# Transposing expert rows in 32 bits, later weight splits, tanh gates and a predicated last stage in a one-core transformer stack

## The reference

```python
# first block: attention with a distance bias, then 16 experts, tw = routing weights (at most 2 of 4 groups, 2 of 4 experts in each)
for e in range(E):
    h = jax.nn.silu(xf @ W1[e]) * (xf @ W3[e])          # 128 -> 512
    out = out + tw[:, e:e + 1] * (h @ W2[e])            # 512 -> 128
# second block: two recurrent layers of width 256 over 126 steps, then a dense layer
    i = jax.nn.sigmoid(g[:, 0 * h_dim:1 * h_dim])       # g = x_t @ Wx + b + h @ Wh
    f = jax.nn.sigmoid(g[:, 1 * h_dim:2 * h_dim])
    c_tilde = jnp.tanh(g[:, 2 * h_dim:3 * h_dim])
    o = jax.nn.sigmoid(g[:, 3 * h_dim:4 * h_dim])
    m_new = jnp.tanh(g[:, 4 * h_dim:5 * h_dim])
    c_new = f * c + i * c_tilde
    h_new = o * jnp.tanh(c_new) + m_new
  return jnp.einsum('bth,ho->bto', h2, Wfc) + bfc
# and 8 experts, one for each token
idx = jnp.argmax(logits, axis=-1)
for e in range(num_experts):
    h = jax.nn.relu(xf @ W1[e] + b1[e])                 # 128 -> 256
    y = h @ W2[e] + b2[e]                               # 256 -> 128
    out = jnp.where((idx == e)[:, None], y, out)
```

## Time and profile before

| | us |
|---|---|
| three timed runs | 1154.62, 1159.3, 1160.98; median 1159.3 |
| profiled execution | 1149.07, its span 1147.2 |
| granted clock of PE, mean of the span | 0.902 of 2.4 GHz |
| busy: PE, DVE, ACT, POOL | 916.4, 834.9, 627.2, 351.2 |
| routing | 176 to 247 |
| tile loop | 247 to 513 |
| gathering and mixing the experts' rows | 513 to 540 |
| recurrence, dense layer | 540 to 1003, 1003 to 1014 |
| last stage | 1014 to 1147 |

### The profile page before, as it was taken

The page is one execution under the profiler, slowest core; times in us unless marked ns, Lnnn a source line. Parts: engine busy times, 40 slices in busy tenths (PEclk is TensorE's granted clock), DMA queues, the critical chain, the costliest instruction groups (busy, mean ns, idle before and its releaser), DMA issues.

```text
span 1147.2 us, 44932 instructions
## 1 busy us (share of the span) xinstructions
PE 916.4 (80%) x17542; PEld 726.7 (63%) x17542; DVE 834.9 (73%) x2906; ACT 627.2 (55%) x1954; POOL 351.2 (31%) x483
## 2 busy tenths in 40 slices
PE   4767777258878778874599999999999999689887
PEld 1346545135555545552589899898899888646665
DVE  3458975986666665666788888888888888646998
ACT  0446668226666666653355555555555555436775
POOL 0326646766666655640000000010000010011221
PEclk9768987559999999995699999999999999778999
DMA  8600014202222211216000000000000000003231
GB/s 239 252 1 2 1 44 151 59 21 61 63 63 65 61 49 52 40 35 168 2 4 0 0 0 0 0 0 0 0 0 0 0 0 0 2 1 129 91 112 51
DMA packets 26713, 52.13 MB, mean 45 GB/s; under 512 B 4529, under 2 KB 17817, under 8 KB 26649
## 3 DMA queue, kind: packets, MB, share of 16 engines
q1 hardware_dynamic: 21656, 41.04, 10.9%
q0 software_dynamic: 4992, 10.23, 3.4%
HBM read 44.02 MB, written 7.24 MB: 45 GB/s over the span
## 4 chain that ended last, share of the span: by engine, by line
PE 30%; DVE 13%; issue 11%; ACT 0%; DVEq 0%; POOL 0%; DMA 0%; POOLq 0%; ACTq 0%
PE quad L1332 18%; PE bank L1332 7%; DVE hidL L1711 4%; DVE post L1471 3%; DVE post L1507 2%; DVE area L1725 1%; DVE post L1513 1%; DVE post L1508 1%; PE quad L1392 1%; PE quad L1342 1%; PE quad L1616 1%; PE bank L1627 0%; PE bank L341 0%; PE bank L1621 0%; PE quad L319 0%
## 5 line engine op out<-in xcount | busy, mean ns | idle before, releaser
L1332 PE MATMUL quad<-post,area 128*128 128x32 f16 (+1 forms) x7520 | 231.6, 183 | 29.6 <-DVE post L1513 22.9
L1332 PEld LDWEIGHTS quad<-post,area 128*128 128x128 f16 x7520 | 214.3, 97 | 44.4 <-DVE post L1513 44.4
L1332 PE MATMUL bank<-post,area 128*128 128x32 f16 (+1 forms) x6260 | 193.5, 180 | 6.3 <-DVE post L1513 4.1
L1332 PEld LDWEIGHTS bank<-post,area 128*128 128x128 f16 x6260 | 177.2, 96 | 12.0 <-DVE post L1513 4.6
L1410 ACT ACTIVATE post<-post 128x64 f32<-128x64 f32 x252 | 64.6, 257 | 160.5 <-DVE post L1471 160.5
L1315 POOL COPY post<-post 128x32 f32 (+1 forms) x126 | 26.5, 210 | 386.2 <-DVE post L1513 386.2
L856 POOL DMA_INDIRECT y_scratch<-area x78 | 85.3, 1094 | 80.1 <-DVE area L1216 66.2
L1497 DVE SCALAR_TENSOR_TENSOR post<-post 128x32 f32<-128x32 f32 x252 | 48.5, 192 | 75.2 <-ACT post L1421 75.2
L937 PE MATMUL quad<-const,area 128*128 128x128 f16 x624 | 55.1, 221 | 48.0 <-DVE area L1203 34.2
L851 POOL DMA_INDIRECT area<-x_scratch,area x78 | 81.8, 1049 | 27.6 <-issue 22.2
L937 PEld LDWEIGHTS quad<-const,area 128*128 128x128 f16 x624 | 40.3, 98 | 78.7 <-DVE area L1203 40.5
(11 more groups left out here) (258 smaller groups left out, 2150.7 us busy)
## 6 DMA issues: line engine op xcount, KB each, us to landing
w0s<-in_w SPq DMA_DIRECT2D x12, 768.0 KB, 12.0
area<-mask_scratch SPq DMA_DIRECT2D x7, 1008.0 KB, 4.7
area<-in_rec SPq DMA_DIRECT2D x7, 640.0 KB
post<-y_scratch SPq DMA_DIRECT2D x16, 252.0 KB
area<-in_w SPq DMA_DIRECT2D x4, 768.0 KB
post<-in_f SPq DMA_DIRECT2D x8, 256.0 KB, 4.5
area<-in_patches SPq DMA_DIRECT2D x1, 1488.4 KB
area<-in_taps SPq DMA_DIRECT2D x1, 1350.0 KB
```

What stands on the lines that cost most here:

```text
L1332: mm = pe.matmul(at[0][:, at[1] + out.start:at[1] + out.stop], rec_w[:, w, s, m * P:(m + 1) * P], operand, start=False, stop=False, skip_g ...
```

## The change

- **Tile loop.** `hid` is transposed as it is, in 32 bits: four transposes in place of eight, into one of two banks by turns. ACT writes the high half from PSUM (`high`), and DVE the low half as PSUM minus the high half (`low`), both straight to `hidT`. ACT's L1014 and DVE's L1210 are gone, and `low` reads PSUM.
- **Late splits.** Experts 12 to 15 are split inside the tile loop, behind tiles 2, 5, 8 and 11, all by ACT and DVE; PE waits for them before tile 32. The recurrent weights' splits start at tile 14 in place of 6, each in two instructions for an engine in place of one, because the columns of the gates i and f get half the scale. `rows_low` moves into the table loop.
- **Gates.** sigmoid(x) is taken as (1 + tanh(x/2))/2, with the halving in weights and bias: one tanh of 96 columns in place of a sigmoid of 64 and a tanh of 32. The cell is kept doubled.
- **Dense layer.** Three of its four blocks are multiplied inside the last steps of the recurrence (`connect`, `FC_AFTER`).
- **Last stage.** The mask product is gone. `down` adds up only over one expert; when a block is done, DVE copies it by predicate, under the token mask, to `xn` (`pick_own`, 32 copies). Bias products are added to the stream apart. The mask's transposes come behind the first three `up`. Block results are added to the stream as they come (`finish`).

```diff
@@ tile loop, PE @@
-                for s, (ready, turned, name) in enumerate((("hid_high", "turned0", "turned_ps0"),
-                                                           ("hid_low", "turned1", "turned_ps1"))):
...
+                pe.wait_ge(sg("gated"), i + 1)
+                if i >= 2:
+                    pe.wait_ge(sg("hid_low"), i - 1)
+                for c in range(C0):
+                    mm = pe.transpose(hidT_bank[i % 2][:, c * P:(c + 1) * P], hid[:, i % 2, c * P:(c + 1) * P], ident)
+                mm.then_inc(sg("turned_ps0"), 1)
             def down(i, weights):
-                pe.wait_ge(sg("turned0"), BATCH + i + 1)
-                pe.wait_ge(sg("turned1"), BATCH + i + 1)
+                pe.wait_ge(sg("hid_low"), i + 1)
@@ tile loop, DVE @@
             def low(i):
                 dve.wait_ge(sg("hid_high"), i + 1)
-                if i >= 2:
-                    dve.wait_ge(sg("turned_ps1"), BATCH + i - 1)
-                dve.tensor_tensor(hid16[:, i % 2, 1, :], hid[:, i % 2, :], hid16[:, i % 2, 0, :], ALU.subtract
+                dve.tensor_tensor(hidT[:, i % 2, 1, :], hidT_bank[i % 2], hidT[:, i % 2, 0, :], ALU.subtract
@@ splits, ACT and DVE @@
-            for e in range(2 * EARLY, E0):
-                w_high(act, e)
...
+                if late_tile(i) is not None:
+                    w_high(act, late_tile(i))
...
-            for e in LOW_DVE[3:]:
-                w_low_dve(dve, e)
-            rows_low(0)
-            rows_low(1)
...
-                if c == 8 or c == 16:
-                    rows_low(2 + c // 16)
+                if c % 4 == 0 and c < 4 * NBLK:
+                    rows_low(c // 4)
@@ recurrence @@
+        FC_AFTER = {SEQ - 1: ((0, 0),), SEQ + 1: ((0, 1),), SEQ + 2: ((1, 0), (1, 1)), SEQ + 3: ((2, 0), (2, 1))}
...
-                act.activation(gates[:, l, SIG:2 * SW], pre[:, l, 0:2 * SW], ACT.Sigmoid, scale=UNSCALE)
-                act.activation(gates[:, l, CAND:CAND + SW], pre[:, l, 2 * SW:3 * SW], ACT.Tanh, scale=UNSCALE
+                act.activation(gates[:, l, 0:3 * SW], pre[:, l, 0:3 * SW], ACT.Tanh, scale=UNSCALE
@@ last stage, DVE @@
-                    dve.tensor_tensor(fhid[:, k % 2, :], relu[:, k % 2, :], blk(mask_b[:, u], k // C1), ALU.mult
-                                      ).then_inc(sg("masked"), 1)
...
+            def pick_own(e, j, u, half):
...
+                dve.wait_ge(sg("f_down"), e * ITEMS1 + (j + 1) * C1)
...
+                dve.copy_predicated(xn_blocks[j], blk(mask_b[:, u], j).bitcast(I32), bank[j][:, 0:BLK]
+                                    ).then_inc(sg("picked"), 1)
...
+                    if k in (5, 7):
+                        pick_own(e, (k - 5) // 2, u, half)
...
+                    if k in (1, 3) and not first:
+                        pick_own(e - 1, (k + 3) // 2, 1 - u, half + u - 1)
```

More of the change, by code:

```diff
@@ L1232, in ffn_dve @@
                 if 1 <= i <= NT:
-                    turned_low(i - 1)
+                    low(i - 1)
+                if late_tile(i - 1) is not None:
+                    w_low_dve(dve, late_tile(i - 1))
                 w = rec_tile(i - 1)
@@ L1420, in cell_of @@
                 act.wait_ge(sg(f"cell{l}"), n)
[L1421 removed]
+                act.activation(tanh_c[:, l], gates[:, l, CELL:CELL + SW], ACT.Tanh, scale=0.5).then_inc(sg(f"tanh_c{l}"), 1)
             def both(t, u):
@@ L1555, in build @@
         ITEMS1 = NBLK * C1
+        LN4_BANKS = [bank[i] for i in (*FC_BANK, 4)]
         ln4_high, ln4_low = split_x("ln4")
@@ L1640, in expert @@
                     n = e * ITEMS1 + k
+                    if first and k == LAG:
+                        turn_mask()
                     if k == 0:
@@ L1678, in expert @@
                         act.wait_ge(sg("f_bias"), e + 1)
+                    if first and k == LAG:
+                        mask_rows()
                     act.wait_ge(sg("f_up"), n + 1)
-                    if not (first and k < 2):
-                        act.wait_ge(sg("masked"), n - 1)
-                    act.activation(relu[:, k % 2, :], bank[4 + k % 4][:, 0:BLK], ACT.Relu,
+                    if not (first and k < 4):
+                        act.wait_ge(sg("f_hid_low"), n - 3)
+                    act.activation(relu[:, k % 4, :], bank[4 + k % 4][:, 0:BLK], ACT.Relu,
                                    bias=f_bias[:, u, c:c + 1]
@@ L1732, in last_dve @@
-            for j in range(NBLK):
-                dve.tensor_tensor(st_blocks[j], st_blocks[j], bank[j][:, 0:BLK], ALU.add).then_inc(sg("final"), 1)
+            for j in range(NBLK // 2, NBLK):
+                pick_own(E1 - 1, j, 1, E1 // 2 - 1)
+                finish(j)
         block = ctx.enter_context(nc.Block())
```

196 lines of the change are left out of this document (108 added, 88 removed).

## The result

Four executions gave 1110.15 to 1119.23 us, median 1117.6, against 1158.94 for the kernel before (four executions): the ratio is 0.9636 (95% interval 0.9592 to 0.968), some 41 us less by the medians. The profiled execution took 1110.15 us, its span is 1108.2.

What follows compares the result with a forecast made beforehand. PE was taken as the nearest bound in the tile loop and recurrence, DVE as ahead in routing and last stage. 6.8 + 30 + 1 + 5 + 8.1 = 51 us off the median 1159.3 gave 1108, range 1085 to 1142.

Steps and rivals of the forecast that it cites:

- Tile loop: Tile loop: 32-bit transposes remove PE's 33.9 us wait behind DVE's low half; net of splits 30 us less.
- a sign of being wrong that I had named: Tile loop: gated products staying 3.2 us apart or more, with idle time put down to "remote" before ACT's high half.
- The first rival: Tile loop: the wait moves and the pace mostly stays; 10 of 34 us won, splits take 4, total 1132; chance 0.20.
- PE's order costs nothing: Tile loop: PE's transposes cost the same, half as many of the dearer 32-bit ones coming to about 0.5 us.
- Late splits: Tile loop: four splits of 1.75 us on DVE, partly hidden by its slack, cost 4 us, between 2.6 and 7.
- The later recurrent splits: Tile loop: the same work in more instructions, covered by DVE's and ACT's slack, cost 0.
- Routing: Before the tile loop: chain 6.2 us earlier, L1116 1.5 shorter, row halves charged 0.9; 6.8 us less, between 5 and 8.
- Recurrence: Recurrence: one tanh saves only in the first and last four passes; 1 us less, between 0 and 2.
- Dense layer: Behind the recurrence: twelve of 16 records move into PE's idle time in the last steps; 5 us less, 2.6 to 6.8.
- the half clock: Dense layer: if the half clock stays for the records put into the last steps, only 2.6 us is left.
- Last stage: Last stage: head 2, end 1.1, and 5 of PE's 8.9 us wait behind DVE's low part; 8 us less, 3 to 12.
- The copy's low price: Last stage: each copy by predicate costs DVE 0.67 us; the rival price of 1.35 gives total 1113, chance 0.05.

Runs made afterwards that it cites:

- the pieces: Changed kernel with every weight split of the tile loop cut into three pieces in three successive tiles; 1063.6 us, 0.9684 of the kernel before.
- the last two groups: Eight follow-up runs on one further chip, among them both unchanged kernels; there the kernel before took 1098.7 us and the changed kernel 1070.8.
- the experiment: Changed kernel with the last stage of before (masked products, mask's transposes and bias products first, four adds at the end); 1086.2 us, 0.9884 of the kernel before.

## Why the prediction was right, and where it was not

**The total and its sign.** 1117.6 lies in the range (1085 to 1142), 10 us above the forecast. It came out near by two errors of opposite sign, which is luck: the tile loop gave 5 us in place of 30, and the other stages 34 in place of 21. The profile met a sign of being wrong that I had named: the starts are 3.24 us apart in the mean, over 3.2, with idle time put down to "remote", though ahead of ACT's token copy and of `keep` and not of ACT's high half.

**Tile loop, the step that failed.** I read PE's 33.9 us of idle time behind DVE's low half as the price of where `low` stood, and took them all off. The same kernel shows what it was: on a chip without held releases its loop takes 204.3 us, so that some 50 of its 255 us were held releases, which surfaced mostly at that wait. The changed kernel has them too and pays them at the next wait, `keep`: 47.6 us. The first rival had this mechanism and, for the loop, its size (10 won, 4 for the splits, 6 net; 5.4 measured); its total of 1132 missed by what the other stages gave. What the transposes are worth by themselves is 5 to 8 us where nothing is held, and most of it lies beside the splits: a recurrent weight's three tiles take 8.7 us with the 32-bit transposes (3.0, 3.0, 2.7) and 9.2 in the kernel before (3.2, 3.3, 2.7), while the undisturbed pace is 2.5 in both; on the first chip they were not tried apart from the splits. That PE's order costs nothing was right: 2.50 us a tile undisturbed, 2.51 before.

**Late splits.** In the loop 6.6 us, not 4, near the upper side: the term left out ACT's half, which delays the silu of one tile, while DVE's half delays the next. The slack was the right measure, as the pieces showed. The later recurrent splits, which I put at 0, cost about as much in either placement, 1.2 us each (intervals of 3.0, 3.0 and 2.7 in place of 2.5). With what they save ahead of the loop, they are neutral where nothing is held.

**Routing.** 6.2 us for the chain and 1.5 for L1117 were exact: 7.8 us between two steps became 1.6, and 1.66 us became 0.17. The row halves cost some 0.4 in the table loop and not the 0.9 I charged: from L1104 to the first gated product the net is 7.3. Another 3.9 us lie ahead of L1104, where the diff changes nothing. On the chip of the last two groups, in executions of kernels that are equal up to there, the places start anywhere from 199.2 to 204.9 us, so I count these 3.9 as the execution's own and not as the change's. That is argued and not shown; the changed kernel's other executions on the first chip, 1116.4 to 1119.2 us, fit it.

**Recurrence.** 1 us forecast, 2.3 and 1.9 measured on two chips, of which the single tanh has 0.9 at most. The steady part does not feel it, as argued from PE's busy time. The rest may lie in the last passes, where PE's steps now run at a granted clock of 1.00 (982 to 987 us) and not 0.50 (999 to 1003 before); that was not tried alone.

**Dense layer.** 5 us forecast, 6.4 measured (6.9 on the other chip). I feared the half clock for what was put in the gaps; in the end the opposite held: with the dense records filling PE's idle time the granted clock was 0.76 from 975 to 982 us and 1.00 from there on.

**Last stage.** 8 us forecast, 14 measured; the experiment gives 15. The copy's low price was right (0.73). Of PE's 8.9 us behind `low` I kept 4 for POOL's splits, but all of it went, since DVE, busy 68 of 88 us, has slack for the stretched low parts. They go on being stretched, by 0.32 and 0.72 us at each of six splits, 6.2 us in all. By the Trainium skill ("SBUF — State Buffer", section "SBUF: two separate sides") a DVE instruction with two SBUF inputs and a GpSimd one that reads SBUF exclude each other for a whole instruction; the trace agrees in that each stretched low part lies beside an instruction of POOL's split. But PE doesn't wait for that. The head gave 4.4 in place of 2: the mask's transposes took 2.25 us in place of 3.25 and the bias products 3.64 in place of 4.09, the clock, which I had left out of the sum; the remaining 0.9 us I can't place.

**Open.** What holds PE's releases on the first chip. The kernels that leave out gathers and address loads could show nothing on a chip where none are held, and no further run was on the first chip. That both traces there turn even a few us behind the last gather (475.3 us in the changed kernel, 491.4 before) points at the gathers, but this is a coincidence in time and no test.

## What to carry to other kernels

Where a wait is put down to "remote", or an engine starts long after its releaser's record has ended, the idle time may belong to whatever holds the signal: here moving the wait moved the loss and did not remove it, and the gain has to be worked out from the pace that the engines could keep. A long auxiliary operation in a pipelined loop costs what exceeds the slack of a tile, at each place again; cut to pieces that fit the slack it is nearly free. And a product of masks for each item can be replaced by one copy by predicate for each block, at the price of an ordinary pass.

## What was not expected of the hardware

- The same two kernels take 1159 and 1118 us on one chip, 1099 and 1071 on another. In the profiled executions the difference is nearly that of one stage, the tile loop (255 and 249 us against 204 and 206). In it, on the one chip, engines that wait for PE start up to 2.5 us after the matmul's end, together, once PE has stopped. The change's ratio depends on it: 0.9636 against 0.9754.
- A copy by predicate of 128 x 504 32-bit values from PSUM takes 0.73 us, a subtraction of 128 x 512 with a PSUM operand 0.68.
- The same four bias products (eight records) took 3.6 us in nine of ten executions with dense products ahead of the mask's transposes and 4.9 in the tenth; with the transposes first they took 3.8, 4.1, 7.1 and 7.1.
